# Rows of maxima of the grouped items issued one place earlier in TensorE's step

## The chip, the cores and the metric

The kernel runs on one core of one Trainium2 chip. The metric is the device time of one execution in microseconds.

## The reference

Four attention layers run one after the other on `x` (4 batches of 512 queries, 256 channels); keys and values of all four come from the same context (4 batches of 1024 keys, 512 channels). Layers 0, 2 and 3 have 16 heads of 64 channels and a bias on a few key columns. Layer 1 is the one that the change touches: its input is RMS-normed, and its 16 query heads of 16 channels share 4 key and value heads.

```python
xn = rmsnorm(x, norm_w)
q = (xn @ wq).reshape(B, T, N_HEADS, HEAD_DIM)
k = (cond @ wk).reshape(B, S, N_KV_HEADS, HEAD_DIM)
v = (cond @ wv).reshape(B, S, N_KV_HEADS, HEAD_DIM)
qg = q.reshape(B, T, N_KV_HEADS, n_rep, HEAD_DIM)
scores = jnp.einsum('btgrd,bsgd->bgrts', qg, k) * scale
attn = jax.nn.softmax(scores.astype(jnp.float32), axis=-1).astype(q.dtype)
out = jnp.einsum('bgrts,bsgd->btgrd', attn, v).reshape(B, T, N_HEADS * HEAD_DIM)
return residual + out @ wo
```

## The kernel before

Operands are split into a high and a low float16 part, so that a product is three matmuls of float16. The work is cut into 112 pairs: in layers 0, 2 and 3 a pair is two heads of one batch, in layer 1 (the grouped layer) it is one key head with its four query heads, of one batch. Pairs 32 to 47 are the grouped ones (`G0` is 32, `G1` is 48); batches go fastest, so every fourth step starts a new key head and with it new weights. The program goes through steps, one for each pair. Every engine has its own program (`group_slot` on TensorE, ScalarE and VectorE for the grouped steps), written out by hand, and runs it in that order; semaphores join them.

A grouped step s has 16 places i. At place i TensorE issues:

- `maxima(s + 1, i)` (line 1000): two matmuls of the next pair's queries with its keys into one of the two halves of the PSUM tile `ps_st`; VectorE reduces each to the negated maxima `nmg` (line 2053).
- `group_scores` (line 1082): the two score matmuls of 128 keys and two heads into the PSUM tile `ps_sm`, of which there is one. Places 0 to 3 do scores 12 to 15 of pair s - 1, places 4 to 15 scores 0 to 11 of pair s. A score waits (`s_exp`) for the exponential of the score ahead of it, which ScalarE takes out of `ps_sm` into `pt` (line 1596).
- other work behind the score: `group_attend` (line 1095) at even places, `project_out` (line 917), `sums`, `rows_of_reciprocals`, the projections of the next pairs.

The maxima of pair s reach its scores in four moves. VectorE's `both_halves(s)` (line 2072) joins them at the end of step s - 1. ScalarE's `columns_of_maxima(s)` (line 1636) spreads them over the columns of `ext_q` at place 0, behind its exponential of that place, and signals `s_nm16`. TensorE's `rows_of_maxima(s, tile)` (line 1009) turns them into rows: four matmuls with the identity matrix for each of the two tiles (two heads each), into a bank of the PSUM tile `ps_j`. VectorE's `group_rows(s, tile)` (line 2079) adds these rows to the queries of that tile and signals `s_tile`; scores 0 and 1 of the pair wait for tiles 0 and 1.

`ps_j` has two banks. A table (`bank_users`) names their users in order, and `take` makes TensorE wait until the user ahead of it in the same bank has been read. In grouped steps from 34 on, bank 1 goes from `out1` of pair s - 2 to `nm0` and then `nm1` of pair s:

```python
        if s > G0 + 1:
            then("out1", s - 2, 1)
        then("nm0", s, 1)
        then("nm1", s, 1)
```

So the first rows wait for `add_out(s - 2, 1)` on VectorE (line 2108, semaphore `s_x`), which stands behind the reduction of `maxima(s + 1, 0)`; its products (`project_out(s - 2, 1)`) are TensorE's last work of place 0. The second rows wait for `group_rows(s, 0)`. Before, the rows stand at places 2 and 3, behind the score and the attend of that place.

Of the kernel before, what the change touches and what calls it, by code (L numbers as in the profile page):

```python
# [30 lines left out]
G0, G1 = STARTS[1], STARTS[2]  # L31
# [26 lines left out]
def grouped(p):  # L58
    return G0 <= p < G1
# [62 lines left out]
def rms_batch(s):  # L122

    b = s - (G0 - 2)
    return b if 0 <= b < B else None
# [245 lines left out]
def build(nc, a, out):  # L371
    with ExitStack() as ctx:
# [492 lines left out]
        def _(pe):  # L865
# [138 lines left out]
            def rows_of_maxima(p, tile):  # L1004
                pe.wait_ge(s_nm16, p + 1)
                dst = take(f"nm{tile}", p)
                for t in range(QT):
                    cols = nmg_w[:, t, 2 * tile:2 * tile + 2, :] if grouped(p) else nm_w[:, t]
                    last = MM(dst[:, t * P:(t + 1) * P], cols.rearrange("p h n -> p (h n)"), ident[:], start=True,  # L1009
                              stop=True)  # L1010
                last.then_inc(s_nm, 1)
# [327 lines left out]
            def first_group_slot():  # L1339

                s = G0
                maxima(s, 8)
                maxima(s, 9)
                attend(s - 1, 1)
                maxima(s, 10)
                maxima(s, 11)
                project_k(s + 2, 0, 0)
                maxima(s, 12)
                project_k(s + 2, 0, 1)
                maxima(s, 13)  # L1350
                mean_squares(rms_batch(s))
                maxima(s, 14)
                sums(s - 1)
                maxima(s, 15)
                project_v(s + 1, 0, range(0, 2))

            def group_slot(s):
                first, last = s == G0, s == G1 - 1
                if first:
                    first_group_slot()  # L1360
                for i in range(20 if last else 16):
                    if not last:
                        maxima(s + 1, i)
                    elif i < 16 and i % 2 == 0:
                        maxima(s + 1, i // 2)
                    if i >= 4:
                        group_scores(s, i - 4)
                    elif not first:
                        group_scores(s - 1, 12 + i)
                    if i < 8 and i % 2 == 0 and not first:  # L1370
                        group_attend(s - 1, 4 + i // 2)
                    if first:
                        if i == 1:
                            rows_of_maxima(s, 0)
                            project_v(s + 1, 0, range(2, 4))
                            rows_of_maxima(s, 1)
                        if i == 4:
                            project_v(s + 1, 1)
                        if i in (5, 6):
                            project_k(s + 2, 1, i - 5)  # L1380
                        if i >= 8 and i % 2 == 0:
                            group_attend(s, i // 2 - 4)
                        if i in (9, 11):
                            project_out(s - 1, i // 11)
                        if i == 12:
                            project_q(s + 2, 0)
                        if i == 14:
                            project_q(s + 2, 1)
                        if i == 15:
                            mean_squares(rms_batch(s + 1))  # L1390
                        continue
                    if i == 0 and s > G0 + 1:
                        project_out(s - 2, 1)
                    if i in (2, 3):
                        rows_of_maxima(s, i - 2)
                    keyed = has_values(s + 2)
                    if i in (4, 5) and keyed:
                        project_k(s + 2, 0, i - 4)
                    if i == 7:
                        sums(s - 1)  # L1400
                    if i in (7, 8) and keyed:
                        project_k(s + 2, 1, i - 7)
                    if i >= 8 and i % 2 == 0:
                        group_attend(s, i // 2 - 4)
                    if i == 9 + keyed:
                        rows_of_reciprocals(s - 1)
                    if i == 10 + keyed:
                        if has_values(s + 1) and not last:
                            project_v(s + 1, 0)
                        if early_bias(s) is not None:  # L1410
                            bias_matrix(early_bias(s))
                    if i == 11 + keyed:
                        project_q(s + 2, 0)
                    if i == 12 + keyed and has_values(s + 1) and not last:
                        project_v(s + 1, 1)
                    if i == 13 + keyed and grouped(s + 2):
                        project_q(s + 2, 1)
                    if i == 15:
                        project_out(s - 1, 0)
                    if last and i == 16:  # L1420
                        project_out(s - 1, 1)
                    if last and i == 17:
                        project_v(s + 1, 0)
                if last:
                    group_attend(s, 6)
                    project_v(s + 1, 1)
                    rows_of_maxima(s + 1, 0)
                    group_attend(s, 7)
# [511 lines left out]
        def _(dve):  # L1940
# [134 lines left out]
            def group_rows(p, tile):  # L2075

                dve.wait_ge(s_nm, queries(p) + 1 + tile)
                q = queries_in(p, tile)
                V.scalar_tensor_tensor(q, bank(f"nm{tile}", p), flag(FLAG_GM), q, ALU.mult, ALU.add).then_inc(s_tile, 1)
# [186 lines left out]
            def group_slot(s):  # L2266
                first, last = s == G0, s == G1 - 1
                if first:
                    maxima(s, 8)
                    maxima(s, 9)  # L2270
                    second_half(s - 1)
                    for u in range(10, 15):
                        maxima(s, u)
                    keys_lo(s + 2, 0)
                    maxima(s, 15)
                    both_halves(s)
                keyed = has_values(s + 2)
                for i in range(16):
                    if first:
                        if i == 2:  # L2280
                            group_rows(s, 0)
                            group_rows(s, 1)
                        if i == 8:
                            keys_lo(s + 2, 1)
                        if i == 13:
                            queries_lo(s + 2)
                        if i == 15:
                            queries_lo(s + 2, 1)
                        if i == 12:
                            add_out(s - 1, 1)  # L2290
                        maxima(s + 1, i)
                        if i in (4, 5):
                            reciprocal(s - 1, i - 4)
                        if i == 10:
                            add_out(s - 1, 0)
                        continue
                    if i in (3, 4):
                        group_rows(s, i - 3)
                    if i == 6 and keyed:
                        keys_lo(s + 2, 0)  # L2300
                    if i == 9 and keyed:
                        keys_lo(s + 2, 1)
                    if i == 12 + keyed:
                        queries_lo(s + 2)
                    if i == 14 + keyed and grouped(s + 2):
                        queries_lo(s + 2, 1)
                    if not last:
                        maxima(s + 1, i)
                    elif i % 2 == 0:
                        maxima(s + 1, i // 2)  # L2310
                    if i == 0 and s > G0 + 1:
                        add_out(s - 2, 1)
                    if i == 5 and (s - 1) % B == 0:
                        wo_lo(set_of(s - 1))
                    if i == 7:
                        reciprocal_by_query(s - 1)
                if not last:
                    both_halves(s + 1)
                if not first:
                    add_out(s - 1, 0)  # L2320
                if s % B == 0:
                    weights_lo(set_of(s) + 1)
                if last:
                    add_out(s - 1, 1)
                    extra_rows(s + 1)
# [110 lines left out]
```

## Time and profile before

| | |
|---|---|
| Median of 3 runs | 3416.62 us (3416.29 to 3416.98) |
| The profiled execution | 3416.71 us, of which 3414.9 us are the span of the trace |
| TensorE (PE) busy | 3294.7 us, 96% of the span |
| VectorE (DVE), ScalarE (ACT), GpSimd (POOL) busy | 2531.0, 2184.4, 2512.9 us |
| Mean granted TensorE clock | 0.997 |

The span runs from the first instruction to the last, and the profiled execution's own time is 1.8 us longer. In the rows PE is TensorE's matmuls and PEld its weight loads, which overlap them. "x2" says that two equal instructions are merged into one row. The two matmuls of a score or of maxima use 64 rows each and run side by side. Times in a timeline are microseconds from the start of the span.

### The profile page before, as it was taken

The numbers are of one execution on the slowest core, as the hardware profiler recorded it, in microseconds if no ns is written. First come the engines' busy times: TensorE is split into PE (matmuls) and PEld (weight loads), VectorE is DVE, ScalarE is ACT, GpSimd is POOL, SyncE is SP. The second block draws the span as 40 slices with busy tenths as digits, with TensorE's granted clock in tenths as the row PEclk, the third lists the DMA queues.
The fourth block names the chain that finished last, engine by engine and source line by source line (L and its number), as shares of the span: only waits on it lengthen the run. The fifth ranks groups of instructions, "written<-read, shape, count | busy, mean of one in ns | idle before, by whom it ended". The sixth has DMA issues, their size and how long they took to land.

```text
span 3414.9 us, 72963 instructions
## 1 busy us (share of the span) xinstructions
PE 3294.7 (96%) x28066; PEld 1559.2 (46%) x28066; DVE 2531.0 (74%) x4668; ACT 2184.4 (64%) x2690; POOL 2512.9 (74%) x1218
## 2 busy tenths in 40 slices
PE   6999999999998898889999999999999999999998
PEld 3445544445443322234454455444444554444553
DVE  6677777777767788856787777777667777777776
ACT  5466666666546777764666666666546666666665
POOL 6888888888752000128888888888888888888887
PEclk9999999999999999999999999999999999999999
DMA  4000000000000000000000000000000000000000
GB/s 156 3 11 11 2 11 11 11 1 9 6 10 13 10 9 17 17 1 11 11 9 3 11 11 2 11 11 11 1 11 11 1 11 11 11 1 11 3 2 26
DMA packets 50195, 42.29 MB, mean 12 GB/s; under 512 B 4928, under 2 KB 42176, under 8 KB 49856
## 3 DMA queue, kind: packets, MB, share of 16 engines
q1 hardware_dynamic: 49136, 37.08, 3.6%
q8 instruction: 231, 3.78, 0.5%
q14 instruction: 108, 0.88, 0.1%
q10 hardware_dynamic: 720, 0.53, 0.1%
HBM read 32.36 MB, written 2.10 MB: 10 GB/s over the span
## 4 chain that ended last, share of the span: by engine, by line
PE 90%; ACT 3%; DVE 2%; issue 2%; POOL 2%; DMA 0%; SPq 0%; ACTq 0%; DVEq 0%; POOLq 0%
PE ps_j L917 40%; PE ps_st L1068 14%; PE ps_j L1108 11%; PE ps_j L1121 6%; PE ps_sm L1000 6%; PE ps_st L1053 3%; PE ps_j L1095 3%; ACT pt L1596 2%; PE ps_sm L1082 2%; PE ps_j L1154 1%; PE ps_st L1000 1%; POOL acc L754 1%; PE ps_j L1009 1%; PE ps_j L1170 1%; PE ps_j L1145 0%
## 5 line engine op out<-in xcount | busy, mean ns | idle before, releaser
L754 POOL TENSOR_TENSOR acc<-acc,pt 128x1024 f32<-128x1024 f32 x570 | 1366.3, 2397 | 261.1 <-ACT pt L1596 207.5
L1596 ACT ACTIVATE pt<-ps_st 128x1024 f32<-128x1024 f32 x768 | 742.7, 1019 | 301.0 <-PE ps_st L1068 289.1
L2063 DVE CUSTOM_DVE_ANT_0 ps_sm<-ps_sm,bias_m,nmx 128x512 f32<-128x512 f32 x666 | 479.8, 756 | 184.7 <-PE ps_j L1000 148.9
L917 PE MATMUL ps_j<-w_h,ctx_h 128*128 128x128 f16 x3072 | 531.5, 220 | 2.3 <-ACT rinv L1612 1.1
L917 PE MATMUL ps_j<-w_h,ctx_l 128*128 128x128 f16 x3072 | 530.5, 219 | 0.0
L917 PE MATMUL ps_j<-w_l,ctx_h 128*128 128x128 f16 x3072 | 530.5, 219 | 0.0
L2063 DVE CUSTOM_DVE_ANT_0 ps_sm<-ps_sm,bias_m 128x512 f32<-128x512 f32 x486 | 334.6, 707 | 160.5 <-PE ps_j L1000 147.8
L1108 PE MATMUL ps_j<-pt,v 128*64 128x512 f32 x1792 | 409.2, 598 | 0.0
L783 POOL TENSOR_TENSOR o_un<-o_un,rinv 128x512 f32<-128x512 f32 x111 | 142.2, 1281 | 320.0 <-ACT rinv L1608 294.5
L2100 DVE RECIPROCAL rinv<-rinv 128x256 f32<-128x256 f32 x190 | 331.1, 1745 | 14.1 <-ACT rinv L1612 4.4
L2053 DVE TENSOR_REDUCE nmg<-ps_st 128x2 f32<-128x1024 f32 x248 | 295.9, 1218 | 43.7 <-PE ps_st L1000 42.5
L917 PEld LDWEIGHTS ps_j<-w_h,ctx_h 128*128 128x128 f16 x3072 | 300.7, 98 | 55.8 <-issue 40.3
L1596 ACT ACTIVATE pt<-ps_sm 128x1024 f32<-128x1024 f32 x256 | 261.3, 1021 | 98.3 <-PE ps_sm L1082 98.2
L917 PE MATMUL ps_j<-ctx_h,w_h 128*128 128x512 f16 x800 | 304.4, 381 | 17.3 <-DVE w_l L1951 13.2
L1573 ACT ACTIVATE p_h<-pt 128x1024 f16<-128x1024 f32 x312 | 319.6, 1052 | 0.0
L917 PEld LDWEIGHTS ps_j<-w_l,ctx_h 128*128 128x128 f16 x3072 | 301.1, 98 | 10.7
L917 PE MATMUL ps_j<-ctx_l,w_h 128*128 128x512 f16 x800 | 304.2, 380 | 0.0
L917 PE MATMUL ps_j<-ctx_h,w_l 128*128 128x512 f16 x800 | 304.1, 380 | 0.0
L1000 PE MATMUL ps_sm<-k_h,q_h 64*128 64x512 f16 x1160 | 293.7, 380 | 9.3 <-DVE nmx L2063 6.9
L917 PEld LDWEIGHTS ps_j<-w_h,ctx_l 128*128 128x128 f16 x3072 | 301.0, 98 | 0.0
L766 POOL TENSOR_TENSOR sq<-acc,sq 128x1024 f16<-128x1024 f32 x92 | 198.7, 2160 | 117.6 <-ACT sq L1603 117.6
L1068 PE MATMUL ps_st<-q_h,k_h 64*128 64x512 f16 x1488 | 282.9, 377 | 0.0
(200 smaller groups left out, 6592.8 us busy)
## 6 DMA issues: line engine op xcount, KB each, us to landing
w_raw<-wk SPq DMA_DIRECT2D x25, 256.0 KB, 2.8
pt<-ctx_t SPq DMA_DIRECT2D x6, 1024.0 KB, 7.3
w_raw<-wv SPq DMA_DIRECT2D x24, 256.0 KB, 3.6
wo_raw<-wo SPq DMA_DIRECT2D x28, 128.0 KB, 2.0
w_raw<-wq SPq DMA_DIRECT2D x24, 128.0 KB, 3.0
k_h<-k_l SPq DMA_DIRECT2D x72, 32.0 KB, 2.0
x<-x_t SPq DMA_DIRECT2D x4, 512.0 KB, 8.5
acc<-ctx_t SPq DMA_DIRECT2D x2, 1024.0 KB, 8.4
```

The lines of the kernel that those rows point to most:

```text
L754: G.tensor_tensor(total, first, pt[:, n % RING, :], ALU.add).then_inc(s_acc, 1)
L766: G.tensor_tensor(acc_l, acc[:, p % 2, :], acc_h, ALU.subtract).then_inc(s_acc_l, 1)
L917: done = MM(dst, l, r, start=first and i == 0, stop=last and i == n - 1)
L1000: last = MM(dst[h], queries_in(p, tile)[d, t * P:(t + 1) * P], k_h[d, r, half * HALF:(half + 1) * HALF], start=True, stop=True)
L1068: last = MM(ps_st[:, side, h, :], k[d, r, keys], q[d, r, :], start=False, stop=n == 2)
L1108: last = MM(dst[h * HD:(h + 1) * HD, :], values_of(p)[:, kt, h * HD:(h + 1) * HD], pt[:, (units(p) + kt) % RING, h * TQ:(h + 1) * TQ], sta ...
L1121: last = MM(dst[h * HD:(h + 1) * HD, :], v[:, p % 2, kt, h * HD:(h + 1) * HD], weights[:, h * TQ:(h + 1) * TQ], start=start, stop=stop)
L1573: A(p_h[:, kt, :], pt[:, n % RING, :], ACT.Copy).then_inc(s_p_h, 1)
L1596: A(pt[:, n % RING, :], src.rearrange("p h q -> p (h q)"), ACT.Exp).then_inc(s_exp, 1)
L2053: V.tensor_reduce(nmg[:, half, t, 2 * tile:2 * tile + 2], maxima_in(p, u), AX_X, ALU.max, negate=True).then_inc(s_max, 1)
L2063: last = V.tensor_tensor_reduce(out=src, in0=src, in1=bias_m[:, t, half * HALF:(half + 1) * HALF], scale=-1.0, scalar=nmx[:, 0, t, h:h + 1 ...
L2100: V.reciprocal(r, r).then_inc(s_rinv, 1)
```

## The change

In steps 34 to 47 the rows of tile 0 move from behind the attend of place 2 to place 1, between that place's maxima and its score. The rows of tile 1 move from place 3 to place 2, behind the score and the attend there. On VectorE `group_rows` moves from places 3 and 4 to places 2 and 3, each time ahead of that place's reduction. Steps 32 and 33 stay as they are.

```diff
--- before.py
+++ after.py
@@ -1363,6 +1363,8 @@
                         maxima(s + 1, i)
                     elif i < 16 and i % 2 == 0:
                         maxima(s + 1, i // 2)
+                    if i == 1 and s > G0 + 1:
+                        rows_of_maxima(s, 0)
                     if i >= 4:
                         group_scores(s, i - 4)
                     elif not first:
@@ -1391,8 +1393,10 @@
                         continue
                     if i == 0 and s > G0 + 1:
                         project_out(s - 2, 1)
-                    if i in (2, 3):
-                        rows_of_maxima(s, i - 2)
+                    if i == 3 - (s > G0 + 1):
+                        rows_of_maxima(s, 1)
+                    if i == 2 and s <= G0 + 1:
+                        rows_of_maxima(s, 0)
                     keyed = has_values(s + 2)
                     if i in (4, 5) and keyed:
                         project_k(s + 2, 0, i - 4)
@@ -2294,8 +2298,8 @@
                         if i == 10:
                             add_out(s - 1, 0)
                         continue
-                    if i in (3, 4):
-                        group_rows(s, i - 3)
+                    if i - 3 + (s > G0 + 1) in (0, 1):
+                        group_rows(s, i - 3 + (s > G0 + 1))
                     if i == 6 and keyed:
                         keys_lo(s + 2, 0)
                     if i == 9 and keyed:
```

Behind line 1365 the lines of the changed kernel are 2 higher than before, behind line 1397 they are 4 higher: VectorE's 2053 is its 2057, 2079 is 2083, 2108 is 2112.

TensorE in step 38 before, from the score of place 2 to the second rows (ps_sm rows are scores 14 and 15 of pair 37, L1095 the attend, L1009 the rows of maxima, ps_st rows the maxima of pair 39):

```order
L1082 MATMUL ps_sm<-q_h,k_h 128x512 [waits s_exp]
L1082 MATMUL ps_sm<-q_h,k_h 128x512
L1095 MATMUL ps_j<-pt,v 32x512 [waits s_ones,s_exp]
L1095 MATMUL ps_j<-pt,v 32x512 x3
L1009 MATMUL ps_j<-ident_sb,ext_q 128x128 [waits s_x,s_nm16]
L1009 MATMUL ps_j<-ident_sb,ext_q 128x128 x3
L1000 MATMUL ps_st<-k_h,q_l 128x512 [waits s_max,s_q_l,s_kb]
L1000 MATMUL ps_st<-k_h,q_l 128x512
L1082 MATMUL ps_sm<-q_l,k_h 128x512 [waits s_exp]
L1082 MATMUL ps_sm<-q_l,k_h 128x512
L1009 MATMUL ps_j<-ident_sb,ext_q 128x128 [waits s_tile,s_nm16]
L1009 MATMUL ps_j<-ident_sb,ext_q 128x128 x3
```

The same part of the changed kernel, which begins one place earlier, behind the maxima of place 1 (the first score is 13, the second 14):

```order
L1009 MATMUL ps_j<-ident_sb,ext_q 128x128 [waits s_x,s_nm16]
L1009 MATMUL ps_j<-ident_sb,ext_q 128x128 x3
L1082 MATMUL ps_sm<-q_l,k_h 128x512 [waits s_exp]
L1082 MATMUL ps_sm<-q_l,k_h 128x512
L1000 MATMUL ps_st<-k_h,q_h 128x512 [waits s_max,s_q_l,s_kb]
L1000 MATMUL ps_st<-k_h,q_h 128x512
L1082 MATMUL ps_sm<-q_h,k_h 128x512 [waits s_exp]
L1082 MATMUL ps_sm<-q_h,k_h 128x512
L1095 MATMUL ps_j<-pt,v 32x512 [waits s_ones,s_exp]
L1095 MATMUL ps_j<-pt,v 32x512 x3
L1009 MATMUL ps_j<-ident_sb,ext_q 128x128 [waits s_tile,s_nm16]
L1009 MATMUL ps_j<-ident_sb,ext_q 128x128 x3
```

The first four matmuls of L1009 have gone from behind the attend to ahead of score 13, with their wait for `s_x` and `s_nm16`; the second four, with their wait for `s_tile`, have gone from behind score 15 to behind the attend.

VectorE in the same step before, from `add_out(36, 1)` (L2108) on:

```order
L2108 SCALAR_TENSOR_TENSOR x<-ps_j,x 128x512 [waits s_x,s_out]
L2053 TENSOR_REDUCE nmg<-ps_st 128x2 [waits s_max_mm] x2
L2079 SCALAR_TENSOR_TENSOR q_h<-ps_j,flags_sb,q_h 128x512 [waits s_nm]
L2053 TENSOR_REDUCE nmg<-ps_st 128x2 [waits s_max_mm]
L2079 SCALAR_TENSOR_TENSOR q_l<-ps_j,flags_sb,q_l 128x512 [waits s_nm]
```

And in the changed kernel:

```order
L2112 SCALAR_TENSOR_TENSOR x<-ps_j,x 128x512 [waits s_x,s_out]
L2057 TENSOR_REDUCE nmg<-ps_st 128x2 [waits s_max_mm]
L2083 SCALAR_TENSOR_TENSOR q_h<-ps_j,flags_sb,q_h 128x512 [waits s_nm]
L2057 TENSOR_REDUCE nmg<-ps_st 128x2 [waits s_max_mm]
L2083 SCALAR_TENSOR_TENSOR q_l<-ps_j,flags_sb,q_l 128x512 [waits s_nm]
L2057 TENSOR_REDUCE nmg<-ps_st 128x2 [waits s_max_mm] x5
```

Each of the two updates of queries (L2079, now L2083) stands one reduction of maxima earlier. ScalarE's, GpSimd's and SyncE's programs keep their order.

## Rows read from the trace of the kernel before

**Rows 1.** The page: the chain that ended last, shares of the span by engine.
```profile
PE 90%; ACT 3%; DVE 2%; issue 2%; POOL 2%; DMA 0%; SPq 0%; ACTq 0%; DVEq 0%; POOLq 0%
```

**Rows 2.** Windows: length, busy us (count) of PE, PEld, DVE, ACT, POOL; clock; DMA.
```profile
1101.00:1510.00 409.00, 362.40 (x2503) 117.04 (x2501) 320.49 (x363) 296.15 (x341) 43.99 (x34) 0.99 0.05 12
1220.00:1247.00 27.00, 24.57 (x171) 7.83 (x170) 22.93 (x25) 20.45 (x24) 2.43 (x2) 1.00 0.03 8
```

**Rows 3.** Timeline of step 38: start, us, engine, line, instruction [idle before <-releaser].
```profile
1221.83 1.05 ACT L1636 ACTIVATE ext_q<-nmx 128x1024 f16<-128x1024 f32 x1
...
1222.69 0.39 PE L1000 MATMUL ps_st<-k_h,q_l 64*128 64x512 f16 x2
1222.86 0.68 DVE L2108 SCALAR_TENSOR_TENSOR x<-ps_j,x 128x512 f32<-128x512 f32 x1
1222.92 0.38 PE L1082 MATMUL ps_sm<-q_l,k_h 64*128 64x512 f16 x2
...
1223.34 1.02 ACT L1596 ACTIVATE pt<-ps_sm 128x1024 f32<-128x1024 f32 x1 [0.46 <-PE ps_sm L1082]
...
1224.42 0.39 PE L1082 MATMUL ps_sm<-q_h,k_h 64*128 64x512 f16 x2 [0.90 <-ACT pt L1596]
...
1225.74 0.40 PE L1009 MATMUL ps_j<-ident_sb,ext_q 128*128 128x128 f16 x4
1226.07 0.39 PE L1000 MATMUL ps_st<-k_h,q_l 64*128 64x512 f16 x2
1226.17 0.75 DVE L2079 SCALAR_TENSOR_TENSOR q_h<-ps_j,flags_sb,q_h 128x512 f16<-128x512 f32 x1 [0.37 <-PE ps_j L1009]
1226.29 0.38 PE L1082 MATMUL ps_sm<-q_l,k_h 64*128 64x512 f16 x2
1226.71 1.02 ACT L1596 ACTIVATE pt<-ps_sm 128x1024 f32<-128x1024 f32 x1 [0.84 <-PE ps_sm L1082]
...
1227.07 0.38 PE L1009 MATMUL ps_j<-ident_sb,ext_q 128*128 128x128 f16 x4 [0.40 <-DVE q_h L2079]
1227.39 0.39 PE L1000 MATMUL ps_st<-k_h,q_h 64*128 64x512 f16 x2
...
1227.79 0.39 PE L1082 MATMUL ps_sm<-q_h,k_h 64*128 64x512 f16 x2
...
1249.99 0.38 PE L1082 MATMUL ps_sm<-q_l,k_h 64*128 64x512 f16 x2
```

**Rows 4.** Line 1009 over the whole run: what its engine sat idle for (us, times).
```profile
  DVE q_h L2079: 6.6, 15
```

**Rows 5.** Timeline of step 37, then of step 45.
```profile
1193.93 1.05 ACT L1636 ACTIVATE ext_q<-nmx 128x1024 f16<-128x1024 f32 x1
...
1194.09 0.39 PE L1082 MATMUL ps_sm<-q_l,k_h 64*128 64x512 f16 x2 [1.16 <-ACT pt L1596]
...
1195.95 0.61 PE L1082 MATMUL ps_sm<-q_h,k_h 64*128 64x512 f16 x2 [1.25 <-ACT pt L1596]
...
1200.71 0.39 PE L1082 MATMUL ps_sm<-q_h,k_h 64*128 64x512 f16 x2
...
1422.41 0.39 PE L1082 MATMUL ps_sm<-q_h,k_h 64*128 64x512 f16 x2 [1.22 <-ACT pt L1596]
...
1425.78 0.39 PE L1082 MATMUL ps_sm<-q_h,k_h 64*128 64x512 f16 x2
```

**Rows 6.** Windows: the half-clock stretch of step 37.
```profile
1196.00:1199.00 3.00, 3.00 (x16) 0.70 (x18) 0.44 (x2) 1.02 (x1) 0.00 (x0) 0.50 0.00 0
```

**Rows 7.** Timeline of step 47.
```profile
1481.17 0.39 PE L1082 MATMUL ps_sm<-q_l,k_h 64*128 64x512 f16 x2
...
1482.68 0.39 PE L1082 MATMUL ps_sm<-q_h,k_h 64*128 64x512 f16 x2 [0.90 <-ACT pt L1596]
...
1482.89 0.69 DVE L2108 SCALAR_TENSOR_TENSOR x<-ps_j,x 128x512 f32<-128x512 f32 x1
...
1486.18 0.38 PE L1082 MATMUL ps_sm<-q_h,k_h 64*128 64x512 f16 x2
```

## The prediction

> **What bounds the kernel now.** First the chain that ended last on the page, to see which engine the end hangs on: TensorE holds 90% of it [rows 1]. An average over the whole program doesn't say what a place in a step is worth, so next the windows of the grouped stage, to see how much room TensorE has there: in 409 us it is busy for 362.40, in the 27 us of one plain step for 24.57, at a granted clock of 1.00 [rows 2]. About a tenth of the stage is TensorE waiting, and the change can gain or lose only there. Then the timeline of one plain step, to see what the waits are for [rows 3]. A score fills the only score tile, ScalarE empties it, and only then may the next score start. Score 13 starts at 1222.92, its exponential at 1223.34 for 1.02 us, score 14 at 1224.42 after TensorE sat idle for 0.90: a loop of 1.50 us from score to score, 0.06 of it between the exponential's end and the next matmul. Where TensorE has more than 1.50 us of work between two scores it sets the pace: from 14 to 15 it is 1.87 (score, attend, rows, maxima). Where it has less, the exponential does: from 15 to score 0 of the new pair it is 1.50 again, and 0.40 of waiting for `group_rows` lies inside. The same score is at 1249.99 one step later, so a step takes 27.07 us. What to look for in these rows: which of two things that end close together comes last.
>
> **The change, part by part.** Nothing is added or removed: in each of 14 steps (34 to 47) two groups of four matmuls and their weight loads on TensorE, and two updates on VectorE, change places. None of them issues a DMA, and the programs of SyncE, GpSimd and ScalarE keep their order.
>
> *Rows of tile 0, from behind the attend to ahead of score 13.* They bring two waits along. The columns on ScalarE are ready at 1221.83 + 1.05 = 1222.88, which alone would cost nothing: score 13 is at 1222.92. The other wait is for the bank, that is for `add_out(s - 2, 1)` on VectorE, which runs from 1222.86 to 1223.54 [rows 3]. From VectorE's end to a TensorE matmul that waits for it the step shows 0.15 us (update until 1226.92, rows at 1227.07). So the rows start at 1223.69. They take 0.33 of TensorE (1225.74 to the maxima at 1226.07), and score 13 starts at 1224.02 in place of 1222.92: **1.10 us later**. TensorE stands meanwhile, since everything else is queued behind the rows: score 13, the maxima of place 2, score 14, the attend. ScalarE waits for score 13 with its next exponential. Before, the same rows had their bank long free.
>
> *Rows of tile 1, from behind score 15 to the old place of tile 0.* Score 14 still follows 13 by the loop of 1.50, and the same 0.33 of rows still lies between 14 and 15, so score 15 keeps its distance of 1.87. What is taken away is the second rows behind score 15, with their wait of 0.40. They ran while ScalarE was at exponential 15 (1226.71 to 1227.73), and score 0 followed at 1227.79. Taking them away gives back nothing: the exponential is late next, at the same distance. The moved rows wait for `group_rows(s, 0)`, now early enough: VectorE reaches it behind one reduction (about 1224.7), ends near 1225.4, and the rows' turn is at 1225.74 + 1.10.
>
> *`group_rows` on VectorE, each one reduction earlier.* I cost this at nothing. What hides it is VectorE's room of 27 - 22.93 = 4.1 us in a step [rows 2]; the second update makes it wait some 0.6 us for the second rows, with the reduction of maxima 3 queued behind it. TensorE needs that reduction only two maxima later. Were that room gone, the price would be at most that 0.6 us a step.
>
> *Does the rest of the step win the 1.10 back?* From score 0 on every wait in the step is for the score loop or for something that TensorE issued itself; all of it moves along. I take the whole 1.10.
>
> *Sum.* Ten plain steps (34, 35, 36, 38, 39, 40, 42, 43, 44, 46): 10 x 1.10 = 11.0 us. In steps 37, 41 and 45, the first behind a new set of weights, ScalarE is late and the columns come last: 1193.93 + 1.05 + 0.06 = 1195.04, plus 0.33 is 1195.37, against score 13 at 1194.09 [rows 5]: 3 x 1.28 = 3.8 us. In step 47 VectorE runs the first maxima of the next layer ahead of `add_out`, which ends at 1482.89 + 0.69 = 1483.58 [rows 7]; plus 0.15 and 0.33, score 13 is at 1484.06 against 1481.17. From there 1.51 to score 14, 1.87 less 0.22 to score 15 (no maxima at odd places in this step; 0.22 is the distance from the maxima at 1226.07 to score 15), 1.50 to score 0: 1488.72 against 1486.18, 2.5 us, since here a wait for `group_rows` did end last. Together **17.3 us**. The profiled execution took 3416.71 us (span 3414.9), 0.09 above the median of 3416.62, so both give **3434 us**, 0.5% more.
>
> *Ends of what the trace can't show.* The bank's wait is the doubtful price. If only the columns counted, the plain step would lose 1222.94 + 0.33 - 1222.92 = 0.35, and the sum would be 3.5 + 3.8 + 2.5 = 9.8 us: 3426.5. I take 1.10, because this wait stands in the program and its row ends 0.66 behind the columns. The other is the clock. In step 37 TensorE was idle for 1.16 and 1.25 us around score 13, and from then the granted clock was 0.50, that is 1.2 of 2.4 GHz [rows 5, 6]; scores 14 to 0 took 4.76 us there and 3.37 in step 45 (1422.41 to 1425.78), so such a fall costs 1.39. Step 41 has one too, step 45 none. The change makes the idle time in these three steps and in step 47 longer. I count the two falls unchanged; the ends are none left, -2.8, and two more, +2.8.
>
> **The rivals.** *The clock falls in every changed step.* For it: a plain step would hold two idle times close together, some 0.6 us ahead of the rows and 0.9 behind the maxima of place 2. Against it: it holds 0.90 and 0.40 now, at a clock of 1.00 [rows 2, 3], and the falls came with 1.16 and 1.25. Price: 14 x 1.39 - 2.8 = 16.7 us more, 3451. The Trainium skill (TensorE: Matmul & The Clock Gate, section "A second HAM failure mode: psum-queue depth-cycling") describes this: a loop that goes through PSUM banks and lets TensorE idle briefly between groups of matmuls has its clock swing between the two levels and pays for it between bursts. By that rule the time would be these 3451 us; the trace agrees in step 37 and not in the plain steps.
>
> *The bank is free in time*, or VectorE gets to `add_out` sooner: 3426.5 as above. For it speaks only that VectorE's turn may shift with TensorE's; against it that the reduction ahead of `add_out` reads maxima of place 0, which nothing in the change moves.
>
> *Not slower: TensorE's waits for `group_rows` end last, and they go.* All waits of this line for it are 6.6 us, 15 times [rows 4]. If they were on the path and score 13 didn't wait, the time would be about 3410.5. This decides if exponential 15 ends before the second rows begin, at 1227.07; it ends at 1227.73 [rows 3], and only step 47 is otherwise.
>
> *The delay is absorbed later in the step*: 3417 or somewhat more. Against it: 24.57 of 27 us are TensorE's own work [rows 2].
>
> **How the numbers follow.** The forecast has 0.77; the fall of the clock everywhere 0.08; the free bank 0.07; the vanished waits 0.05; the absorbed delay 0.03. The range takes the forecast with its ends of the clock (3431 to 3437), some hundredths of a microsecond per step in the hand-over times, one or two falls of the clock in plain steps, and the free bank: 3426 to 3441. A measurement of this kernel can tell 0.2%, 7 us, from no change. The vanished waits come to 6 us, so I put 0.02 of them beyond that bound and 0.03 within; with the absorbed delay: faster 0.02, no change 0.06, slower 0.92.
>
> **What would show it.** In the changed kernel's timeline of a plain step: the first rows start about 0.15 us behind `add_out`'s end, with TensorE idle some 0.6 us ahead of them until line 2112; score 13 comes about 1.3 us behind the maxima of place 1, where it came 0.23 behind; the second rows wait for nothing; TensorE is idle for most of a microsecond ahead of score 0, until the exponential; the step takes 28.2 us. The window of the stage from step 34 to 47 grows by 17 us, and everything behind it keeps its length. I am wrong if score 13 is less than 0.7 us later, if score 0 comes earlier against score 14, or if clocks of 0.50 stand in plain steps.

## The result, and the profile after

| | before | changed kernel |
|---|---|---|
| Median of 4 runs each | 3416.45 us (3414.86 to 3416.98) | 3439.47 us (3435.37 to 3444.89) |
| The profiled execution, and its span | 3416.71, 3414.9 | 3435.37, 3433.6 |
| TensorE, VectorE busy | 3294.7, 2531.0 | 3293.7, 2531.3 |
| Mean granted TensorE clock | 0.997 | 0.996 |

The ratio is 1.0068 with a 95% interval of 1.0055 to 1.008: the change is slower by 23 us, where the prediction had 17.3, and 3439.5 lies near the upper end of its range (3426 to 3441). The work is the same, as the busy times show. The profiled execution is the fastest of the four, and 18.7 us longer than that of before; the rest up to 23 us is scatter between executions, which is larger than before and is taken up below, with e4 and e8.

The chain that ended last has less TensorE in it and more of ScalarE and VectorE [rows 1]. A line of VectorE's reductions (2057) is now among the chain's lines, with 1%:

```profile
PE 88%; ACT 4%; DVE 3%; POOL 2%; issue 2%; DMA 0%; SPq 0%; DVEq 0%; ACTq 0%; POOLq 0%
```

The timeline of the changed kernel: first step 34, then step 37, step 38, which is the step of [rows 3], step 47, and the first rows of the layer behind the grouped stage (start, us, engine, line, instruction, idle before and what ended it; rows are left out, TensorE's own only at "...").

```profile
1099.54 0.38 PE L1082 MATMUL ps_sm<-q_h,k_h 64*128 64x512 f16 x2
...
1104.38 0.39 PE L1082 MATMUL ps_sm<-q_h,k_h 64*128 64x512 f16 x2 [0.91 <-ACT pt L1600]
1104.69 1.87 PE L1095 MATMUL ps_j<-pt,v 128*32 128x512 f32 x8
1106.50 0.61 PE L1009 MATMUL ps_j<-ident_sb,ext_q 128*128 128x128 f16 x4
...
1197.71 0.40 PE L1009 MATMUL ps_j<-ident_sb,ext_q 128*128 128x128 f16 x4 [2.10 <-ACT ext_q L1640]
1198.04 0.39 PE L1082 MATMUL ps_sm<-q_l,k_h 64*128 64x512 f16 x2
...
1199.55 0.39 PE L1082 MATMUL ps_sm<-q_h,k_h 64*128 64x512 f16 x2 [0.90 <-ACT pt L1600]
...
1224.05 1.05 ACT L1640 ACTIVATE ext_q<-nmx 128x1024 f16<-128x1024 f32 x1
...
1224.90 0.39 PE L1000 MATMUL ps_st<-k_h,q_l 64*128 64x512 f16 x2
1225.07 0.68 DVE L2112 SCALAR_TENSOR_TENSOR x<-ps_j,x 128x512 f32<-128x512 f32 x1
...
1225.89 0.38 PE L1009 MATMUL ps_j<-ident_sb,ext_q 128*128 128x128 f16 x4 [0.60 <-DVE x L2112]
1226.21 0.39 PE L1082 MATMUL ps_sm<-q_l,k_h 64*128 64x512 f16 x2
...
1227.72 0.39 PE L1082 MATMUL ps_sm<-q_h,k_h 64*128 64x512 f16 x2 [0.91 <-ACT pt L1600]
1229.04 0.40 PE L1009 MATMUL ps_j<-ident_sb,ext_q 128*128 128x128 f16 x4
...
1229.59 0.38 PE L1082 MATMUL ps_sm<-q_l,k_h 64*128 64x512 f16 x2
...
1231.09 0.39 PE L1082 MATMUL ps_sm<-q_h,k_h 64*128 64x512 f16 x2 [0.91 <-ACT pt L1600]
...
1254.38 0.39 PE L1082 MATMUL ps_sm<-q_l,k_h 64*128 64x512 f16 x2
...
1499.39 0.38 PE L1009 MATMUL ps_j<-ident_sb,ext_q 128*128 128x128 f16 x4 [2.48 <-DVE x L2112]
1499.71 0.39 PE L1082 MATMUL ps_sm<-q_l,k_h 64*128 64x512 f16 x2
...
1501.22 0.61 PE L1082 MATMUL ps_sm<-q_h,k_h 64*128 64x512 f16 x2 [0.91 <-ACT pt L1600]
...
1505.67 0.39 PE L1082 MATMUL ps_sm<-q_h,k_h 64*128 64x512 f16 x2 [0.91 <-ACT pt L1600]
...
1542.90 0.38 PE L1009 MATMUL ps_j<-ident_sb,nm_w 128*128 128x128 f16 x4 [0.78 <-ACT v L1571]
```

In step 38 the first rows wait 0.60 us, until line 2112, VectorE's `add_out`, and start 0.14 behind its end (1225.07 + 0.68 = 1225.75). Score 13 comes 1.31 behind the maxima of place 1, where it came 0.23 behind [rows 3]. The second rows wait for nothing. The same score is at 1254.38 one step later: the step takes 28.17 us, where it took 27.07.

What the rows' line waits for has changed with it; this is the view of line 1009 over the whole run (us, times; idle time that no other instruction ended is left out), against 6.6 us, 15 times, for `group_rows` [rows 4]:

```profile
  ACT ext_q L1640: 23.8, 18
  DVE x L2112: 8.4, 11
  ACT v L1571: 0.8, 1
  DVE q_h L2083: 0.7, 1
```

The first line, the wait for ScalarE's columns, was 1.7 us, 2 times, before. Of its 23.8 us, 16.9 (14 times) belong to the line's weight loads, which overlap other matmuls; the matmuls themselves wait 6.9 us for the columns, 4 times, of which 2.10 us each in steps 37, 41 and 45. The second line is the wait for `add_out`, in the ten plain steps and step 47.

The windows of the changed kernel: the stage, one plain step, and windows around the four stretches in which the clock was low (length, busy us of the engines, granted clock third from the end). Such a stretch, with TensorE's granted clock at 0.50, is called a fall of the clock from here on; but for the one of step 45 the windows are wider than the falls.

```profile
1099.00:1526.00 427.00, 364.11 (x2487) 116.47 (x2485) 319.79 (x358) 293.69 (x337) 42.89 (x33) 0.97 0.04 11
1218.00:1246.20 28.20, 24.51 (x173) 7.81 (x172) 23.11 (x25) 20.58 (x24) 2.43 (x2) 1.00 0.03 8
1104.00:1107.00 3.00, 2.62 (x14) 0.60 (x14) 1.32 (x2) 1.34 (x2) 0.00 (x0) 0.64 0.01 3
1312.00:1321.00 9.00, 6.50 (x34) 1.66 (x38) 5.93 (x7) 4.22 (x6) 0.00 (x0) 0.62 0.22 64
1432.50:1442.50 10.00, 8.62 (x40) 1.53 (x36) 5.69 (x7) 4.26 (x5) 0.00 (x0) 0.50 0.12 33
1500.00:1503.00 3.00, 2.09 (x14) 0.30 (x10) 1.88 (x5) 2.05 (x2) 2.92 (x2) 0.63 0.00 0
```

TensorE's own work in the plain step is the same 24.5 us as in [rows 2]; the step has grown by idle time. The clock of the stage fell from 0.99 to 0.97. The four falls lie in steps 34, 41, 45 and 47; before there were two, in steps 37 and 41.

How long is the stage? In the trace of before, from score 12 of step 34 to the first rows of the next layer:

```profile
1101.53 0.38 PE L1082 MATMUL ps_sm<-q_h,k_h 64*128 64x512 f16 x2
...
1523.40 0.38 PE L1009 MATMUL ps_j<-ident_sb,nm_w 128*128 128x128 f16 x4 [0.78 <-ACT v L1567]
```

That is 421.87 us. In the changed kernel it is 1542.90 - 1099.54 = 443.36, so the stage is **21.5 us longer**. It starts 1101.53 - 1099.54 = 2.0 us sooner; no line ahead of it has changed, and the first matmul of line 1009 in the whole run is already 1.9 sooner (at 47.2, before at 49.1). What is behind the stage is shorter by 21.5 - 2.0 - 18.7 = 0.8. So the whole loss is in the stage, and more of it than the sum of 17.3 says.

### The profile page after: what moved, and what is told of

Its sections match the earlier page's. It is cut to its first block, busy times and chain, and to the rows that moved or that the text cites. A ratio compares the mean times of both kernels' runs of the same rounds, so it can differ in the third digit from the quotient of the medians.

```text
span 3433.6 us, 72963 instructions
## 1 busy us (share of the span) xinstructions
PE 3293.7 (96%) x28066; PEld 1557.0 (45%) x28066; DVE 2531.3 (74%) x4668; ACT 2185.6 (64%) x2690; POOL 2512.4 (73%) x1218
## 4 chain that ended last, share of the span: by engine, by line
PE 88%; ACT 4%; DVE 3%; POOL 2%; issue 2%; DMA 0%; SPq 0%; DVEq 0%; ACTq 0%; POOLq 0%
PE ps_j L917 39%; PE ps_st L1068 13%; PE ps_j L1108 11%; PE ps_j L1121 6%; PE ps_sm L1000 6%; PE ps_st L1053 3%; PE ps_j L1095 3%; ACT pt L1600 2%; PE ps_sm L1082 2%; POOL acc L754 2%; PE ps_j L1154 1%; DVE nmg L2057 1%; PE ps_st L1000 1%; PE ps_j L1009 1%; PE ps_j L1170 1%
```

## The experiments

Each was timed in five rounds (5 to 11 executions) beside the kernel before on the same chip; those medians of before were 3416.27 (e1 to e4), 3416.39 (e5 to e8) and 3417.31 us (e9). A ratio is always to the kernel before; the diffs show the lines that matter and leave out the rest. The theory: the first rows are costly because they stand *ahead of a score* and everything in TensorE's order waits with them; the rest of the excess is the clock. The rivals: the second rows' new place, or the bank alone, makes the cost.

**e1: the first rows in the same place of the step, but behind its score** (against the changed kernel):

```diff
-                    if i == 1 and s > G0 + 1:
-                        rows_of_maxima(s, 0)
                     if i >= 4:
...
                         project_out(s - 2, 1)
+                    if i == 1 and s > G0 + 1:
+                        rows_of_maxima(s, 0)
```

> The first rows stand behind score 13 of place 1 in place of ahead of it; the second rows stay at place 2. If the loss is that score 13 stands behind the bank's wait (my theory): the rows fit into TensorE's idle 0.90 us ahead of score 14, score 13 comes 0.23 us behind the maxima of place 1 again, a plain step takes 27.1 us as before, only step 47 loses about 1.3 us, and the time is about 3418 us (3415 to 3420). Rival one, that rows at place 1 cost TensorE's time wherever they stand in it: 14 x 0.33 = 4.6 us more than before, 3421 us. Rival two, that the loss comes from the second rows or from VectorE's updates at their new places: no better than the change, 3435 to 3440 us.

Measured: 3417.79 us (3415.0 to 3419.68), ratio 1.0004 (0.9995 to 1.0012). Its timeline in step 38:

```profile
1225.15 0.38 PE L1082 MATMUL ps_sm<-q_l,k_h 64*128 64x512 f16 x2
1225.91 0.38 PE L1009 MATMUL ps_j<-ident_sb,ext_q 128*128 128x128 f16 x4 [0.38 <-DVE x L2112]
1226.23 0.39 PE L1000 MATMUL ps_st<-k_h,q_h 64*128 64x512 f16 x2
1226.65 0.39 PE L1082 MATMUL ps_sm<-q_h,k_h 64*128 64x512 f16 x2
```

The wait for `add_out` is still there, 0.38 us, and costs nothing: score 14 follows score 13 by 1.50, the loop of the exponential. Moving four matmuls behind the score takes away the loss, but for step 47, where scores 12 to 0 still take 8.31 us against 7.08 before. The wait itself is not what costs; that the score stands behind it is.

**e2: the second rows and VectorE's second update back in their old places, only the first rows ahead** (against the changed kernel; the second `group_rows` goes back to place 4, its lines aren't printed):

```diff
-                    if i == 3 - (s > G0 + 1):
+                    if i == 3:
                         rows_of_maxima(s, 1)
```

> The first rows stay ahead of score 13, the second rows go back to place 3 behind score 15, and VectorE's second update to place 4. My theory: score 13 stays 1.10 us later, but the 0.33 us of rows between scores 14 and 15 go out of the score loop (1.87 becomes 1.54 us), so a plain step takes 27.9 us, 0.33 less than with the change; about 4.5 us less than the change as a whole, 3430 to 3435 us. Rival, that the second rows are what was lost: back to 3417 us. Rival, that they cost nothing in either place: as the change, 3439 us.

Measured: 3433.14 us (3428.43 to 3435.77), ratio 1.0053 (1.004 to 1.0067), as expected. So most of the loss comes from the first rows. In its timeline of step 38 score 15 follows score 14 by 1.54 where the changed kernel has 1.87:

```profile
1226.26 0.39 PE L1082 MATMUL ps_sm<-q_h,k_h 64*128 64x512 f16 x2 [0.91 <-ACT pt L1600]
...
1227.80 0.38 PE L1082 MATMUL ps_sm<-q_l,k_h 64*128 64x512 f16 x2
```

Rows between the attend of place 2 and score 15 cost their own 0.33 us; behind score 15 they are hidden by its exponential.

**e3: both of these** (first rows at place 1 behind the score, second rows at place 3; against the kernel before, VectorE as in e2):

```diff
-                    if i in (2, 3):
-                        rows_of_maxima(s, i - 2)
+                    if i == 1 and s > G0 + 1:
+                        rows_of_maxima(s, 0)
+                    if i == 3:
+                        rows_of_maxima(s, 1)
+                    if i == 2 and s <= G0 + 1:
+                        rows_of_maxima(s, 0)
```

> The first rows behind score 13 of place 1, the second at place 3 behind score 15, VectorE's updates at places 2 and 4: both groups of rows then stand where TensorE waits for the exponential. My theory: score 13 at its old time and 0.33 us less between scores 14 and 15, a plain step of 26.7 us, 13 x 0.33 = 4.3 us less than before, step 47 about 1.1 us more: 3413 us (3410 to 3416), faster than both kernels. Rival, that VectorE or ScalarE sets the step's length: 3416 to 3418 us.

Measured: 3415.51 us (3410.39 to 3416.56), ratio 0.9995 (0.9987 to 1.0004): within the expected range, but faster than the kernel before only by its plain step, not by a total clear of noise. The plain step takes 26.75 us, 0.32 less than before, as forecast; the total gained less than expected. The falls of the clock in the first step behind new weights (37, 41, 45) are still there: executions with a mean clock of 0.999 took 3410.4 to 3410.9, those at 0.997 took 3415.5 to 3416.6.

**e4: the change with TensorE's waits filled.** The maxima matmuls of places 1, 2 and 4 are repeated, writing the same values again, so that TensorE works while it would wait:

```diff
-            def maxima(p, u):
+            def maxima(p, u, again=0):
...
-                for h in range(2):
+                for h in [0, 1] * (again + 1):
...
-                        maxima(s + 1, i)
+                        again = {1: 9 if s % B == 1 else 2, 2: 3, 4: 2}.get(i, 0) if s > G0 + 1 else 0
+                        maxima(s + 1, i, again)
```

> The change as it is, but TensorE repeats the two matmuls of the maxima while it waits: 2 times more at place 1 (9 in the steps behind new weights), 3 at place 2, 2 at place 4, in steps 34 to 46. They write the same values again and lie in waits, so no score moves by them. If what the change lost beyond 17.3 us is falls of TensorE's clock in the longer waits (my theory): no stretch at a clock of 0.50 in steps 34 to 46, rounds that lie within 2 us of each other, and 3430 to 3435 us. Rival, that the waits alone make the whole 23 us and the scatter has another cause: 3437 to 3442 us with rounds as far apart as those of the change (3435 to 3445).

Measured: 3432.81 us (3428.87 to 3434.62), ratio 1.0049 (1.0036 to 1.0062). Its rounds differ by 5.8 us and not by 2, so that part of the expectation missed: step 47 isn't filled and its profile has a fall there, and the runs of before beside it differ by 4.8 (3414.2 to 3419.0). Its score 12 of step 34, the rows and score 14 of step 38, the first rows behind the stage, and the window of steps 34 to 46:

```profile
1101.15 0.38 PE L1082 MATMUL ps_sm<-q_h,k_h 64*128 64x512 f16 x2
...
1226.07 0.38 PE L1009 MATMUL ps_j<-ident_sb,ext_q 128*128 128x128 f16 x4 [0.17 <-DVE x L2113]
...
1227.89 0.39 PE L1082 MATMUL ps_sm<-q_h,k_h 64*128 64x512 f16 x2 [0.26 <-ACT pt L1601]
...
1537.77 0.38 PE L1009 MATMUL ps_j<-ident_sb,nm_w 128*128 128x128 f16 x4 [0.78 <-ACT v L1572]
...
1099.00:1493.00 394.00, 358.35 (x2576) 118.45 (x2574) 309.59 (x328) 279.89 (x322) 36.73 (x30) 1.00 0.05 12
```

The clock is 1.00, where the changed kernel has 0.97 in the same window. The plain step keeps its 28.17 us, its rows still start when `add_out` ends. So this profile prices the places without the clock: its stage takes 1537.77 - 1101.15 = 436.62 us, 14.75 more than before. Before's two falls (2.8 us) are gone and the one in step 47 (1.4) is there, so the places alone cost 14.75 + 2.8 - 1.4 = 16.2. By the medians the extra work makes the kernel 5 to 7 us faster than the change without it (3437.91 and 3439.47). The intervals of the ratios overlap, but each of e4's five executions (3434.62 at most) is below each of the nine of the change (3435.37 at least).

**e5: the waits behind the exponential taken away** (against the kernel before): e3's places in steps 34 to 46, and ScalarE's cast of the output weights (`wo_hi`), which stood ahead of the columns in steps 37, 41 and 45, behind them (only the lines of the cast are printed):

```diff
+                    if i == 2 and s > G0 + 1 and (s - 1) % B == 0:
+                        wo_hi(set_of(s - 1))
...
-                    wo_hi(set_of(s))
+                    if first:
+                        wo_hi(set_of(s))
```

> The kernel before, with the first rows behind score 13 at place 1 in steps 34 to 46 (step 47 stays), VectorE's first update one reduction earlier there, and ScalarE's split of the new output weights (wo_h) moved from the end of steps 36, 40 and 44, where it waits for TensorE's products of place 0 and holds exponential 12 back, to behind the exponential of place 2 of the next step. My theory: 0.33 us less in each of 13 steps, in steps 37, 41 and 45 score 14 comes 0.9 us sooner and no fall of the clock is left (2 x 1.39): 3406 us (3404 to 3411). Rival, that the weights' splits themselves, not the wait, hold ScalarE: 3411 to 3414 us.

Measured: 3406.26 us (3405.13 to 3409.09), ratio 0.9967 (0.9955 to 0.9979), as expected. The window of the stage in its profile has a clock of 1.00, and no fall.

**e6: the bank freed.** As e5, and `out1` of pair s - 2 uses bank 1 *behind* the second rows, at place 3, so that the first rows wait for the columns alone (steps 34 to 45, against the kernel before; `add_out` and `wo_hi` move to place 4; only the bank's table is printed):

```diff
-        if s > G0 + 1:
+        moved = G0 + 1 < s < G1 - 2
+        if s > G0 + 1 and not moved:
             then("out1", s - 2, 1)
         then("nm0", s, 1)
         then("nm1", s, 1)
+        if moved:
+            then("out1", s - 2, 1)
```

> As the run with two waits, and in steps 34 to 45 the products out1 of pair s - 2 move from place 0 to place 3 behind the second rows, their add_out on VectorE to place 4, and the bank's table follows, so that the first rows no longer wait for add_out. My theory: the first rows begin 0.06 us behind the columns and lie behind score 13; the 0.65 us of out1 leave the stretch from score 12 to 13 and fill the wait ahead of score 0; scores 12 to 0 take 0.66 us less than in the kernel before in place of 0.33: 3404 us (3401 to 3408). Rival, that out1 at place 3 pushes score 0 back by all it takes: 3406 to 3410 us.

Measured: 3424.84 us (3423.28 to 3429.48), ratio 1.0023 (1.0014 to 1.0032): 21 us above the expectation, 18.6 above e5, on which it builds, and slower than before. Its timeline in step 38 (lines are 3 higher on TensorE):

```profile
1225.25 0.40 PE L1012 MATMUL ps_j<-ident_sb,ext_q 128*128 128x128 f16 x4 [0.53 <-ACT ext_q L1643]
...
1228.02 0.40 PE L1012 MATMUL ps_j<-ident_sb,ext_q 128*128 128x128 f16 x4
...
1230.11 0.38 PE L920 MATMUL ps_j<-o_h,wo_h 128*128 128x512 f16 x1 [1.70 <-DVE q_l L2089]
```

The first rows are free as intended. But `out1` now takes the bank right behind the second rows, and must wait 1.70 us until VectorE's second update has read them. The bank's wait was moved to its next user, and made longer: the plain step takes 28.04 us, where e5 has 26.75.

**e7: e6 with the first rows ahead of score 13 again** (their line behind the score then leaves these steps out):

```diff
                         maxima(s + 1, i // 2)
+                    if i == 1 and G0 + 1 < s < G1 - 2:
+                        rows_of_maxima(s, 0)
                     if i >= 4:
```

> As the run with the bank freed, but the first rows stand ahead of score 13 again, as in the change. They wait for the columns alone. My theory: ScalarE's columns, 0.06 us of hand-over and 0.33 us of rows stand between exponentials 12 and 13 in place of the columns alone, 0.81 us more in each of 12 steps than with the rows behind the score: 3414 us (3411 to 3417). So being ahead of the score costs even without the bank's wait. Rival, that only the bank's wait was the loss: 3404 to 3406 us, as the run with the bank freed.

Measured: 3435.89 us (3433.85 to 3437.85), ratio 1.0054 (1.0041 to 1.0066). It shares e6's wait, so its total missed too; its difference to e6 is 11.05 us where 9.7 were expected. The first rows wait 0.74 us for the columns there. Its plain step takes 28.79 us against e6's 28.04, 0.75 more where 0.81 were expected; its profile has falls in six steps (36, 37 and 42 to 45), that of e6 in two, so part of the 11.05 is the clock. Standing ahead of the score costs even with the bank free. It is no clean price for the rival of the free bank, since with `out1` gone from place 0 TensorE reaches the rows sooner.

**e8: the change once more**, unedited, beside e5, e6 and e7 on one chip:

> The change once more, beside the others on one chip. If its loss beyond 17.3 us is falls of the clock that come at other places in each execution: rounds scattered over 5 us or more between 3433 and 3445, the longer ones at the lower mean clock. Rival, that the four first runs were an accident of the chip: within 2 us of each other.

Measured: 3437.91 us (3436.26 to 3442.39), ratio 1.0061 (1.0049 to 1.0074), as expected. The times of its five executions go with the clock: 3436.26 twice at 0.996, 3437.91 at 0.995, 3440.64 at 0.994, 3442.39 at 0.993. In its profile the falls are in steps 37, 41, 42, 45 and 46, not in 34 and 47. Step 42 is a plain one; its timeline, and a window behind its waits:

```profile
1345.13 0.38 PE L1009 MATMUL ps_j<-ident_sb,ext_q 128*128 128x128 f16 x4 [0.60 <-DVE x L2112]
...
1346.95 0.39 PE L1082 MATMUL ps_sm<-q_h,k_h 64*128 64x512 f16 x2 [0.90 <-ACT pt L1600]
1347.27 1.90 PE L1095 MATMUL ps_j<-pt,v 128*32 128x512 f32 x8
1349.10 0.61 PE L1009 MATMUL ps_j<-ident_sb,ext_q 128*128 128x128 f16 x4
...
1347.00:1350.00 3.00, 3.00 (x16) 0.69 (x18) 1.16 (x2) 1.02 (x1) 0.00 (x0) 0.56 0.01 3
```

The idle times are those of step 38 above, where the clock stayed at 1.00; here the attend takes 1.90 us instead of 1.07 and the rows 0.61 instead of 0.40.

**e9: e6 with `out1` two places later**, at place 5 (`add_out` at 6, the casts of the output weights behind them), where the bank has long been read (against e6; only TensorE's lines are printed):

```diff
-                        if G0 + 1 < s < G1 - 2:
-                            project_out(s - 2, 1)
+                    if i == 5 and G0 + 1 < s < G1 - 2:
+                        project_out(s - 2, 1)
```

> As the run with the bank freed, but out1 of pair s - 2 at place 5 behind score 1 in place of place 3, add_out on VectorE at place 6, the split of wo_h at place 6 and of wo_l at place 8. In the run with the bank freed TensorE stood 1.70 us ahead of out1, which had become the next user of the bank of the second rows and waited for VectorE's second update. If that wait was all (my theory now): at place 5 the update is long done and out1 fits into the wait ahead of score 2; scores 12 to 0 take 6.5 us in a plain step against 7.3 in the kernel before, and the time is 3402 us (3400 to 3407). Rival, that VectorE falls behind by add_out at its new place, or the sums of place 7 wait for it: 3406 us or more.

Measured: 3397.58 us (3397.47 to 3402.1), ratio 0.9948 (0.9935 to 0.9962), 4 us better than expected, which is below the expected range too, and **20 us faster than the kernel before**. Half of the 20 is e5's, which had 10 without touching the bank. Its timeline in step 38:

```profile
1212.36 0.39 PE L1085 MATMUL ps_sm<-q_h,k_h 64*128 64x512 f16 x2
...
1214.82 0.40 PE L1012 MATMUL ps_j<-ident_sb,ext_q 128*128 128x128 f16 x4 [0.53 <-ACT ext_q L1643]
...
1217.59 0.40 PE L1012 MATMUL ps_j<-ident_sb,ext_q 128*128 128x128 f16 x4
...
1218.77 0.39 PE L1085 MATMUL ps_sm<-q_h,k_h 64*128 64x512 f16 x2 [0.47 <-ACT pt L1603]
...
1220.63 0.39 PE L920 MATMUL ps_j<-o_h,wo_h 128*128 128x512 f16 x1
```

From score 12 to score 0 it takes 6.41 us; the changed kernel takes 8.40 (its score 12 is at 1222.69). `out1` waits for nothing, and the clock of the stage in its profile is 1.00.

## Why the prediction was right in direction, and 6 us short

- **The rows ahead of score 13 wait for the bank: right, and exactly so.** The forecast was 1.10 us a plain step and a step of 28.2; measured are 28.17 against 27.07 in step 38, and 1.08 to 1.10 more in the other plain steps (step 34 holds a fall; in e8, without one, it takes 1.04 more). Of the two waits `add_out` came last, as argued; e1 and e2 put the loss on this one move.
- **Nothing comes back from the second rows: right.** Score 14 to 15 is 1.87 and 15 to 0 is 1.50, as in [rows 3], and the idle time ahead of score 0 is 0.91. The rows in between cost 0.33 in the changed kernel as in the one before; e2 and e3 show that this 0.33 could have been had by leaving the second rows at place 3.
- **`group_rows` earlier on VectorE costs nothing: right.** The second update waits 0.81 us for its rows (forecast some 0.6), and no maxima wait for it in the plain step.
- **Steps 37, 41, 45: the term of 1.28 was too large.** In step 37 the rows wait 2.10 us and score 13 then follows 0.33 behind their start, as worked out; but score 13 to 14 is 1.51 now and was 1.86 [rows 5]. Before, ScalarE's columns delayed the exponential of score 13 as well; now they are over by then. That gives 0.35 back: 0.93 a step, 1 us less in the sum. I had carried the shift of score 13 through to the end without looking at what held score 14.
- **Step 47: right.** Without a fall, in e8's profile, scores 12 to 0 take 9.61 us against 7.08: 2.53, forecast 2.54. In the first profile a fall is added: from score 13 to 0 it takes 1505.67 - 1499.71 = 5.96, in e8 4.67.
- **The clock: the step that failed.** I had written "I count the two falls unchanged; the ends are none left, -2.8, and two more, +2.8". Without falls the places cost 11.0 + 2.8 + 2.5 = 16.3 us. The stage grew by 21.5, and it lost the two falls of before, 2.8; so the falls of this execution cost about 21.5 - 16.3 + 2.8 = 8 us in place of 2.8; that is 5.2 more, beyond the end of 2.8 that I had set. e4, without falls up to step 46, confirms the 16.3. The windows point the same way: length times missing clock is 3 x 0.36 + 9 x 0.38 + 10 x 0.50 + 3 x 0.37 = 10.6 us in the four, where before the whole stage missed some 409 x 0.01 = 4 [rows 2]. My price of 1.39 holds for a fall of some 3 us; the one in step 45 lasted 10 and cost 3.2 (the step takes 33.54 us, in e4 30.30). And the number isn't fixed, so the executions spread from 3435 to 3445, one of the four beyond the range. That the median lies within it is owed to the range's room for falls in plain steps, not to the sum.
- **The rival of the clock** had a chance of 0.08 with a fall in all 14 steps. In number it was wrong, four or five steps of 14; in kind it was partly right, since plain steps are among them (34, then 42 and 46), which my own text named as a sign against the forecast. I had argued that 0.40 and 0.90 us of idle time had been harmless before, and took 0.60 and 0.90 for as harmless. The Trainium skill (TensorE: Matmul & The Clock Gate, section "A second HAM failure mode: psum-queue depth-cycling") has the clock swing in loops that idle briefly between groups of matmuls through PSUM banks; the traces agree in some steps and not in most. e4 fits it: with the idle times filled down to 0.17 and 0.26 us no such stretch is left in steps 34 to 46.
- **The other rivals fell.** The bank was not free in time (its price of 9.8 was worked out too high as well: it kept step 47's 2.5, which is a wait for the bank), the vanished waits for `group_rows` (6.6 us before, 0.7 now) gave nothing, and the step absorbed nothing.

What stays open: why a given execution falls in step 42 and another in step 34, with nearly the same idle times ahead as in steps that keep their clock. And the scatter that is left in e4 wasn't traced to a place outside step 47.

## What to carry to other kernels

On an engine that runs in order, price a move by what stands behind the moved instruction while it waits: the same wait for `add_out` cost 1.10 us a step ahead of a score and nothing behind it, where an exponential was awaited anyway. Follow a shared bank to its next user before freeing it for the first: e6 moved the wait and lost 18.6 us against e5, on which it builds; e9 put the next user two places later and was 8.7 us faster than e5 (on another chip). And where a change adds idle time to TensorE, don't take the number of falls of the clock from the one trace at hand: here two became four or five, at 1.3 to 3.3 us each.

## What the runs showed that was not expected

- The same kernel's executions differ in where the clock falls, and the time goes with it: of the changed kernel's first four, 3435.37 us came at a mean clock of 0.996, 3439.43 and 3439.52 at 0.995, 3444.89 at 0.992.
- Idle times of 0.60 and 0.90 us ahead of one attend were followed by half clock (1.2 of 2.4 GHz) in step 42 of one execution, and by full clock in step 38 of another.
- Repeated matmuls that write the same values again took the falls out of the changed kernel's steps 34 to 46, and all of e4's executions were faster than any of the change: in e4 TensorE is busy for 358.35 of 394 us, where the changed kernel has 337.84 in the same window.
